# Blank rows stored in the stage of experts and projection in place of the attention

## What is computed

```python
x = x + _L0_gnn_ref(_layernorm(x), adj, Wq, Wk)       # attention over adj
x = x + _L0_ffn_ref(_layernorm(x)[None], ...)[0]      # 2 of 8 experts, the same two for all nodes
x = x + _L1_gnn_ref(_layernorm(x), adj, ...)          # weights exp(e) per node, masked by adj
x = x + _L1_ffn_ref(_layernorm(x)[None], ...)[0]      # 2 of 8 experts, chosen by each node
```

```python
_, idx = jax.lax.top_k(x @ Wg + bg, 2)
mask = jax.nn.one_hot(idx, 8).sum(axis=-2)
h = gelu(einsum('td,edh->teh', x, W1) + b1)
out = einsum('ted,te->td', einsum('teh,ehd->ted', h, W2) + b2, mask)
```

## Time and profile before

| | us |
|---|---|
| median of 3 runs | 834.89 |
| lowest and highest run | 834.57, 837.68 |
| span of the profiled execution | 873.3 |

### The profile page before, as it was taken

One profiled execution on the slowest core, in us unless ns is written; L12 is line 12 of the kernel. 1 busy time (PEld: TensorE's weight loads), 2 busy tenths in 40 slices (PEclk: granted clock), 3 DMA queues, 4 the chain that ended last, 5 costly groups with the idle time before them and its releaser, 6 DMA issues. The chain is left out here.

```text
span 873.3 us, 11391 instructions
## 1 busy us (share of the span) xinstructions
PE 723.2 (83%) x3372; PEld 424.4 (49%) x3372; DVE 571.8 (65%) x1658; ACT 491.2 (56%) x741; POOL 196.0 (22%) x233
## 2 busy tenths in 40 slices
PE   2758999999999999999929978799899785776740
PEld 1543444444444444444418966354445374665640
DVE  7785668788888878787864787556555662534325
ACT  1746888888888888888827785222312241222210
POOL 2240000000000000000005531015434456565560
PEclk9969999999999999999958997799999876889875
DMA  4108989899999989887530000401100122222208
GB/s 130 69 0 262 288 260 262 255 273 253 259 258 260 272 249 275 243 255 223 165 128 8 1 2 0 122 5 39 33 25 29 56 67 68 73 79 74 79 18 288
DMA packets 100893, 124.58 MB, mean 143 GB/s; under 512 B 9038, under 2 KB 78930, under 8 KB 100576
## 3 DMA queue, kind: packets, MB, share of 16 engines
q1 hardware_dynamic: 96288, 115.32, 45.9%
q0 software_dynamic: 4544, 8.54, 3.0%
HBM read 88.54 MB, written 36.20 MB: 143 GB/s over the span
## 5 line engine op out<-in xcount | busy, mean ns | idle before, releaser
L552 DVE SCALAR_TENSOR_TENSOR probs<-adj,probs 128x1024 f32<-128x1024 int32 x128 | 156.7, 1224 | 77.0 <-ACT probs L525 68.0
L475 PE MATMUL ps<-x,qT 128*128 128x512 f16 x768 | 188.0, 382 | 3.2 <-PEq L198 3.2
L525 ACT ACTIVATE probs<-ps 128x1024 f32<-128x1024 f32 x128 | 130.9, 1023 | 51.0 <-PE ps L475 51.0
L536 ACT ACTIVATE mask<-probs 128x1024 fp8e4<-128x1024 f32 x128 | 134.0, 1047 | 0.0
L487 PE MATMUL ps<-probs,v 128*128 128x512 f32 x256 | 130.8, 592 | 0.0
L1397 PE MATMUL ps<-mask,parts 128*128 128x512 fp8e4 x512 | 119.7, 391 | 8.1 <-DVE parts L1664 8.1
L475 PEld LDWEIGHTS ps<-x,qT 128*128 128x128 f16 x768 | 75.5, 98 | 94.7 <-issue 5.7
L1571 ACT ACTIVATE mask<-ps,mask 128x256 f32<-128x256 f32 x78 | 32.6, 471 | 101.3 <-PE ps L1482 46.7
L1647 POOL DMA_INDIRECT mixed_spill<-mask,xn x78 | 76.3, 978 | 57.0 <-DVE mask L1794 32.3
L558 DVE TENSOR_TENSOR p_lo<-probs,p_hi 128x512 f16<-128x512 f32 x128 | 87.6, 684 | 0.1
L1600 POOL DMA_INDIRECT sorted_rows_spill<-rows,slots x64 | 62.8, 982 | 99.5 <-issue 54.4
(11 more groups left out here) (289 smaller groups left out, 975.3 us busy)
## 6 DMA issues: line engine op xcount, KB each, us to landing
adj<-in_adj SPq DMA_DIRECT2D x128, 512.0 KB, 4.8
sorted_rows_spill<-blank SPq DMA_DIRECT2D x32, 528.0 KB, 6.7
sorted_rows_spill<-blank SPq DMA_DIRECT2D x26, 198.0 KB, 7.4
xn<-sorted_rows_spill SPq DMA_DIRECT2D x39, 132.0 KB
mask<-mixed_spill SPq DMA_DIRECT2D x8, 512.0 KB, 6.3
mask<-in_x SPq DMA_DIRECT2D x4, 512.0 KB, 5.8
feat_spill<-mask SPq DMA_DIRECT2D x8, 256.0 KB
x_feat<-in_x SPq DMA_DIRECT2D x8, 256.0 KB, 4.8
```

Source lines behind the costliest of these rows:

```text
L475: ins = nc.tensor.matmul(out, qT[:, q_half, j], kT[:, c, k_half * GROUP:(k_half + 1) * GROUP], start=(n == 0), stop=(n == 2))
L525: nc.scalar.activation(probs[:, k % RING, :], ps[:, b:b + 2, :].rearrange("p b n -> p (b n)"), ACT.Exp, scale=1.0 / QK_SCALE ** 2).then_in ...
L536: nc.scalar.activation(mask[:, k * W:(k + 1) * W], probs[:, k % RING, :], ACT.Sign, saturate=False).then_inc(mask_kept, 1)
L552: nc.vector.scalar_tensor_tensor(out=probs[:, k % RING, :], in0=adj[:, k % LOADS, :], scalar=0.0, in1=probs[:, k % RING, :], op0=ALU.is_gt ...
```

## The change

The stores of blank rows leave `attend` with their buffer and semaphores. They are issued in `mix_and_project`, all 58 in a row, after SP's last load of that block; SP then waits until they have landed. POOL makes the blank row at the start of that block. Number, size and content of the stores are the same.

```diff
@@ attend: sync
                 for k in range(STEPS):
-                    if k % 4 == 3:
-                        a = k // 4
-                        if a == 0:
-                            sp.wait_ge(blank_ready, 2)
-                        sp.dma_start(io["sorted"][a * BLANKS:(a + 1) * BLANKS, :].rearrange("(q p) n -> p q n", p=P),
-                                     blank[:, :].unsqueeze(1).to_broadcast([P, BLANKS // P, ROW])).then_inc(blank_out, 16)
-                        if a < TAIL_ROWS // TAIL:
-                            sp.dma_start(io["sorted"][E * N + a * TAIL:E * N + (a + 1) * TAIL, :].rearrange("(q p) n -> p q n", p=P),
-                                         blank[:, :].unsqueeze(1).to_broadcast([P, TAIL // P, ROW])).then_inc(blank_out, 16)
                     c, jp = divmod(k, PAIRS)
...
-                sp.wait_ge(blank_out, 16 * (STEPS // 4 + TAIL_ROWS // TAIL))
@@ attend: gpsimd
-                nc.gpsimd.memset(blank[:, 0:D], 0.0).then_inc(blank_ready, 1)
-                nc.gpsimd.iota(blank[:, D:ROW].bitcast(I32), [[0, ROW - D]], base=2 * N, channel_multiplier=1).then_inc(blank_ready, 1)
@@ mix_and_project
+        BLANK_PIECES = 32
+        BLANKS = E * N // BLANK_PIECES
+        TAIL_ROWS = 2 * P * ROUTED_STEPS
+        TAIL = 3 * P
@@ mix_and_project: sync
                 sp.dma_start(w_last, io["W_node"][D - 1, :].partition_broadcast(P)).then_inc(node_in, 16)
+                sp.wait_ge(blank_ready, 2)
+                for a in range(BLANK_PIECES):
+                    sp.dma_start(io["sorted"][a * BLANKS:(a + 1) * BLANKS, :].rearrange("(q p) n -> p q n", p=P),
+                                 blank[:, :].unsqueeze(1).to_broadcast([P, BLANKS // P, ROW])).then_inc(blank_out, 16)
+                    if a < TAIL_ROWS // TAIL:
+                        sp.dma_start(io["sorted"][E * N + a * TAIL:E * N + (a + 1) * TAIL, :].rearrange("(q p) n -> p q n", p=P),
+                                     blank[:, :].unsqueeze(1).to_broadcast([P, TAIL // P, ROW])).then_inc(blank_out, 16)
+                sp.wait_ge(blank_out, 16 * (BLANK_PIECES + TAIL_ROWS // TAIL))
@@ mix_and_project: gpsimd
                 nc.gpsimd.memset(mean_over, 1.0 / N).then_inc(weights_of_mean, 1)
+                nc.gpsimd.memset(blank[:, 0:D], 0.0).then_inc(blank_ready, 1)
+                nc.gpsimd.iota(blank[:, D:ROW].bitcast(I32), [[0, ROW - D]], base=2 * N, channel_multiplier=1).then_inc(blank_ready, 1)
                 pool.wait_ge(affine_in, 32)
```

More of the change, by code:

```diff
@@ L393, in attend @@
         STEPS = GROUPS * PAIRS
-        BLANKS = E * N // (STEPS // 4)
-        TAIL_ROWS = 2 * P * ROUTED_STEPS
-        TAIL = 3 * P
         TURN_STEP = 1
@@ L424, in attend @@
         epilogue_chain = sem("epilogue_chain")
-        blank = buf("blank", [P, ROW])
-        blank_ready, blank_out = sem("blank_ready"), sem("blank_out")
         with nc.Block() as block:
@@ L691, in mix_and_project @@
         bias = buf("bias", [P, D])
+        blank = buf("blank", [P, ROW])
+        blank_ready, blank_out = sem("blank_ready"), sem("blank_out")
+        BLANK_PIECES = 32
+        BLANKS = E * N // BLANK_PIECES
+        TAIL_ROWS = 2 * P * ROUTED_STEPS
+        TAIL = 3 * P
         DOWN_BANK, UP_BANK, TURN_BANK, ROUTE_BANK = 0, 2, 6, 2
```

## The result

| | before | after |
|---|---|---|
| median, us | 834.74 (4 runs) | 853.65 (4 runs) |
| lowest and highest run, us | 834.57, 837.68 | 851.37, 856.62 |
| span of the profiled execution, us | 873.3 | 851.0 |

The change makes the kernel slower: the ratio is 1.0214, 95% interval [1.0186, 1.0243], or +18.9 us where +10.3 was forecast. It is slower beyond the noise; whether by more than 2% these runs leave open. The traffic left a stage that had never waited for it and did not fit into the stage that it went to.

A forecast was written before the change was run, and what follows sets the result against it. PE was taken to bound the attention, and the stores' landing against DVE's end to decide the next stage: 11.6 us delay less 1.3 us at the attention's start, +10.3 on 834.9, gave 845.2 us; range 832.5 to 860.

The forecast's parts named there:

- What bounds the kernel before: Attention: PE sets the period, 2.8 us a step and 45.71 us a chunk; no transfer sets it, except at the start.
- The start of the attention: Attention, step 3: without stores ahead of it `adj` leaves about 2 us sooner; -1.3 us, with 0 as the other end.
- POOL and the traffic beside the work: Next stage: POOL's memset and iota hidden by its 12.2 us bias wait; traffic slowing the stage priced at 0 to 3 us.
- The meeting point: End of the next stage: all engines meet, so each microsecond the stores land after DVE is done costs one; delay 11.6 us.
- The rate: Stores in the next stage: 22.57 MB at 240 GB/s take 94.0 us; range 206 to 328 GB/s.
- The rival that the stores fit: Next stage: stores land before DVE is done, 833.6 us, not slower; chance 0.34, including misses under 5.5 us.
- The threshold of 274 GB/s: Next stage: the store rate that decides whether the stores land by DVE's end at 546.6; above it they fit.
- The Trainium skill's rule: Next stage: at line rate, about 358 GB/s, the stores would take 63 us and be hidden; the forecast did not adopt it.
- Issuing: Next stage, SP's queue: 58 issues cost 28.8 us, behind the stage's own loads, so no operand of the stage is delayed.
- PE's clock: Start of the last stage: PE is granted 0.50 there already in the kernel before, however long the pause; adds nothing.
- The profile's 38.4 us over the median: Profiled execution, 873.3 us: a stage 4.4% shorter without the profile, about 4 of 98 us, would make the delay grow by 4.
- slow rival: Next stage: stores at 206 GB/s land at 573.8, 27.2 us late, giving 860.8 us; chance 0.14.

The follow-up runs named there:

- The kernel with the late stores: Kernel before, its blank stores kept in the attention but issued every third step from step 17 on; 834.57 us against 836.09, ratio 0.9986.
- fewer stores: Changed kernel with the 26 small stores back in the attention, the 32 large ones left in the next stage; 833.76 us against 834.32, ratio 0.9995.
- 512 B at a distance of 512: Kernel before plus 58 further stores in the stage of experts, 512-byte packets in rows 512 bytes apart, into an unread array; 837.05 us against 834.32.
- 528 B at 576: Kernel before plus 58 further stores in the stage of experts, 528-byte packets in rows 576 bytes apart, into an unread array; 839.89 us against 834.32.

## Why the prediction was right in kind and short in size

**What bounds the kernel before: right.** The attention's period did not move at 0.63, 0.94 or 1.05 of the DMA engines. Only my share for after was off, 0.63 where I wrote 0.75: it fell by a third where the rate fell by a quarter, from the 259 GB/s of the earlier trace rows to 195, since the small packets took more of the engines' time than their part of the bytes.

**The start of the attention: right.** I took -1.3 us; the mask of step 3 waits for ACT alone, and the next stage's first load is issued at 447.47 in place of 448.91, 1.44 us sooner. The kernel with the late stores, which has this part of the change alone, gives 1.6 to 1.8. Not every profile shows as much: from SP's first load of `adj` to its first load of the stage behind, the five profiles with the early stores take 380.95 us on average (380.65 to 381.28), the nine without them 379.21 to 380.27, so 0.7 to 1.7 us less.

**POOL and the traffic beside the work: right.** The stage lasts 96.8 us (447.47 to DVE's 544.22) against 97.7 and 97.1 in the two profiles of before; the bound of 0 to 3 us for a slower stage was not used.

**The meeting point: right.** SP without its wait, larger packets and fewer stores each take the loss away or nearly so, each by another way. What each leaves, or saves, is what the landing (or the last issue) has over DVE.

**The rate: the term that was mis-sized.** I took 240 GB/s from three or four half-microsecond rows; the stretch of 70 us shows 224, within my 206 to 328. The shape that I read there came out: after's stores, once their traffic is up, go at 322 and 305 GB/s (462.5 to 463.5) and are at 218 two microseconds later (465 to 466). The start of the last stage came out 17.4 us later, where I had 11.6 - 1.3 = 10.3. The 7.1 us between them, by the terms of the sum:

| term | forecast | measured | us |
|---|---|---|---|
| first store issued | 460.4 | 460.27 | -0.1 |
| 22.57 MB by the rate | 94.0 at 240 GB/s | 100.8 at 224 GB/s | +6.7 |
| from issue to traffic and from traffic to landing | 1.0 + 1.5 | 104.3 - 100.8 = 3.5 | +1.0 |
| from the last to the first transfers of the next stage | 547.50 - 546.59 = 0.9 | 564.92 - 564.55 = 0.4 | -0.5 |

(104.3 is 564.55 - 460.27.) The last stage adds 1.7, which is inside its spread. 17.4 + 1.7 = 19.1, against 18.9 by the medians. Where the same kernel stored at 250 GB/s, it lost 8.7, less than the 10.3 forecast. So the forecast stands inside what the kernel does, and what it lacked was a spread of the rate from place to place; its own came from one profile.

**The rival that the stores fit: wrong, at two places narrowly.** I gave it, with a miss of under 5.5 us, 0.34, for the weights' load at 303 GB/s. That load is a poor guide to these stores: packets of 528 B were at 185 to 266 GB/s in all kernels, packets of 512 B at a distance of 512 at 287 and those of 2112 B at 378. But 250 and 252 GB/s, on two of the four chips or places, are close to the 257 at which the miss falls under 5.5 us, so the runs do not say that 0.34 was too much. The threshold of 274 GB/s, on the other hand, held: at 261 (528 B at 576) the last stage starts late, at 552.61, and at 287 (with 21.9 MB) the stores land 7.0 us before the others are done.

The Trainium skill's rule, page "DMA: Bandwidth & Descriptors", section Specifications, that 512 B and more run at line rate, does not hold for these stores: 528 B run at 252 GB/s on the chip where 2112 B reach 378, 67% of it, and 512 B at a distance of 512 at 287 on another chip.

**Issuing: a price that I left at 28.8 us** was 97.7. It did not enter the sum, since the landing comes later still; in the kernel without SP's wait it is what is left of the loss.

**PE's clock: right, as far as the traces show.** I wrote that it adds nothing. PE stands 8.1 us before its first matmul of the last stage in the kernel with four rows in a packet, and 49.2 us in that with neighbouring rows on the second chip. From that matmul on, four rows first:

```profile
550.10:554.10 4.00, 3.98 (x10) 1.49 (x11) 3.90 (x7) 1.88 (x3) 0.00 (x0) 0.50 1.16 311
554.10:556.10 2.00, 2.00 (x10) 0.76 (x8) 1.97 (x4) 0.64 (x2) 0.00 (x0) 0.83 1.14 271
```

```profile
590.90:594.90 4.00, 3.95 (x10) 1.47 (x11) 3.88 (x6) 1.85 (x3) 0.00 (x0) 0.50 1.15 314
594.90:596.90 2.00, 2.00 (x11) 0.85 (x10) 1.96 (x4) 0.67 (x2) 0.00 (x0) 0.97 1.22 283
```

The clock starts at 0.50 (1.2 GHz) and rises in both, no later after the long pause, and the last stage lasts 286.6 and 285.7 us.

**The profile's 38.4 us over the median** made me allow for a stage that is some 4% shorter without it. They lay in the last stage of that one execution alone; the allowance had no ground.

**Two slips of the working** change nothing: the 743 KB of the burst are thousands of bytes (726 KB in the unit of the rows), and the range ends at 860 where its slow rival comes to 860.8.

## What to carry to other kernels

An empty stretch of a queue has a size in microseconds, not in bytes: divide the bytes by the rate that these very packets sustain when they queue, taken from the low rows of a burst and with a spread (here 221 to 250 GB/s for the same kernel), and compare the landing with whoever ends the stage now. Where the fit is close, make the packets larger (here 528 to 2112 B, 252 to 378 GB/s on one chip) or move a part (here three quarters fitted whole). And an engine that issues a long row of transfers is held by them until the last issue is out, even if it waits for none of them to land.

## What was not expected of the hardware

- A row of stores paces its own issue: 58 in 97.7 us, where each alone took 0.435 or 0.582 us; at the last issue the remaining stores needed another 6.6 us to land.
- The same kernel stored at 225, 250 and 221 GB/s in three comparisons, while its runs of one comparison agreed within 2.5 us (854.4 to 856.92) and those of another within 5.3 us (851.37 to 856.62).
- A row of stores begins faster than it goes on: 322 GB/s over 462.5 to 463 in after, 218 over 465 to 466, 224 over 470 to 540.
- Packets of 528 B to neighbouring rows went at 185 GB/s, to rows 128 apart at 221, on the same chip.
- Stores of 2112 B from SBUF to HBM held 378 GB/s over 40 us, more than the 303 GB/s that the load of the weights held over four.
